# A graph-network kernel on one core: an order of work by tables, the low halves of a layer's rows on VectorE, and the sync queue in another order

## What is computed

```python
# layer 0: attention with 4 heads of 16, over the neighbours only
scores = einsum('bhnd,bhmd->bhnm', x @ Wself, x @ Wother)
masked = leaky_relu(a * scores, 0.2) / sqrt(16) + where(a == 0, -1e9, 0)
attn = softmax(masked, -1) * (a != 0)
x = layernorm(x + relu(attn @ (x @ Wv) + bias))
# layer 1: mean over the neighbours, adj with one more on the diagonal
x = layernorm(x + (adj + I) @ x / rowsum(adj + I))
# layer 2: adj @ (x @ W) + bias
x = layernorm(x + adj @ (x @ W2) + bias2)
# layer 3: 1 where adj @ x is over 0.5, else 0
t = adj @ x
x = layernorm(x + where(t > 0.5, 1, 0))
```

## Time and profile before

| | us |
|---|---|
| median of 3 runs | 1537.56 (1536.58 to 1537.99) |
| the profiled execution | 1541.21 |
| its span | 1539.1 |

### The profile page before, as it was taken

The page is one execution under the profiler, slowest core; times in us unless marked ns, Lnnn a source line. Parts: engine busy times, 40 slices in busy tenths (PEclk is TensorE's granted clock), DMA queues, the critical chain, the costliest instruction groups (busy, mean ns, idle before and its releaser), DMA issues.

```text
span 1539.1 us, 20977 instructions
## 1 busy us (share of the span) xinstructions
PE 1360.2 (88%) x7296; PEld 683.8 (44%) x7296; DVE 1240.7 (81%) x1490; ACT 1223.2 (79%) x1404; POOL 1053.1 (68%) x562
## 2 busy tenths in 40 slices
PE   4798898999999999999989989998999989799766
PEld 2443344454444444544444544444444444345323
DVE  2779889787979889788887879887788788987864
ACT  1699799887988889788888879888798888888631
POOL 3177768678677767777676786787677776876411
PEclk9999899999999999999999999999899999999977
DMA  6734444243333433343442443344334334101000
GB/s 94 117 34 75 47 87 52 58 39 60 77 44 69 48 67 73 48 58 34 98 51 58 40 62 75 44 74 45 67 55 67 53 37 82 41 15 28 14 11 11
DMA packets 140879, 84.95 MB, mean 55 GB/s; under 512 B 100372, under 2 KB 130522, under 8 KB 140762
## 3 DMA queue, kind: packets, MB, share of 16 engines
q1 hardware_dynamic: 125542, 64.67, 19.7%
q0 software_dynamic: 14160, 18.51, 15.4%
q10 hardware_dynamic: 1072, 0.43, 0.1%
HBM read 103.33 MB, written 21.38 MB: 81 GB/s over the span
## 4 chain that ended last, share of the span: by engine, by line
PE 50%; ACT 12%; issue 12%; DVE 12%; POOL 10%; DMA 2%; SPq 1%; ACTq 0%; POOLq 0%; DVEq 0%
PE M L604 10%; PE Z L570 9%; PE M L659 9%; PE Z L577 8%; POOL LS L503 7%; ACT LS L751 6%; PE Z L588 5%; ACT LS L759 4%; DVE LS L913 3%; PE Z L673 3%; DVE RP L899 3%; PE Z L613 3%; DMA adj_cast<-in_adj_dram 1%; PE Z L727 1%; DVE X L983 1%
## 5 line engine op out<-in xcount | busy, mean ns | idle before, releaser
L503 POOL TENSOR_TENSOR LS<-LS,MB 125x1000 f32<-125x1000 f32 x372 | 867.1, 2348 | 339.2 <-DVE LS L913 272.3
L751 ACT ACTIVATE LS<-Z 126x1000 f32<-126x1000 f32 x576 | 576.8, 1002 | 154.1 <-PE Z L577 153.1
L899 DVE TENSOR_TENSOR RP<-LS,RP 125x1000 f32<-125x1000 f32 x480 | 575.6, 1199 | 84.8 <-ACT LS L751 63.3
L759 ACT ACTIVATE LS<-LS 125x1000 f32<-125x1000 f32 x576 | 596.9, 1037 | 51.9 <-POOL LS L503 32.9
L570 PE MATMUL Z<-AT,BI 126*126 126x500 fp8e4 x1152 | 378.0, 411 | 79.1 <-ACT LS L751 52.5
L577 PE MATMUL Z<-FS,FO 128*125 128x500 f16 x1152 | 356.2, 391 | 0.0
L604 PE MATMUL M<-LS,V 126*18 126x500 f32 x2304 | 317.3, 624 | 5.9 <-ACT LS L759 5.8
L570 PEld LDWEIGHTS Z<-AT,BI 126*126 126x126 bf16 x1152 | 127.7, 142 | 389.9 <-ACT LS L751 187.1
L913 DVE TENSOR_TENSOR LS<-LS,MB 125x1000 f32<-125x1000 f32 x204 | 293.0, 1441 | 5.0
L577 PEld LDWEIGHTS Z<-FS,FO 128*125 128x125 f16 x1152 | 165.8, 144 | 97.4 <-issue 17.6
L659 PE MATMUL M<-AT,XP 125*128 125x500 fp8e4 x756 | 192.9, 377 | 0.0
(11 more groups left out here) (133 smaller groups left out, 811.2 us busy)
## 6 DMA issues: line engine op xcount, KB each, us to landing
MB<-row_maxima SPq DMA_DIRECT2D x48, 500.0 KB, 4.0
adj_cast<-in_adj_dram POOLq DMA_DIRECT2D x96, 183.1 KB, 4.5
FO<-PARTS SPq DMA_DIRECT2D x120, 46.9 KB, 2.2
FS<-PARTS SPq DMA_DIRECT2D x120, 46.9 KB, 2.1
XF<-in_x_dram SPq DMA_DIRECT2D x8, 336.0 KB
XA<-in_x_dram SPq DMA_DIRECT2D x8, 336.0 KB
out_dram<-X SPq DMA_DIRECT2D x7, 375.0 KB
AT<-adj_cast SPq DMA_TRANSPOSE x144, 2.8
```

Source lines behind the costliest of these rows:

```text
L503: nc.gpsimd.tensor_tensor(rows, rows, MB[:P, u % 2, :, :], ALU.subtract).then_inc(sub_pool, 1)
L751: nc.scalar.activation(LS[:PD, q % RL, :, :], banks("Z", q)[:PD], ACT.Prelu, alpha=SLOPE).then_inc(bent, 1)
L759: nc.scalar.activation(rows, rows, ACT.Exp, scale=0.25).then_inc(exps, 1)
L899: nc.vector.tensor_tensor(run, rows, run, ALU.max).then_inc(maxed, 1)
```

## The change

Each event of a graph gets its step from a table. Core of the diff (lines `...` left out):

```diff
-LAG = 18
-SUB_AT = LAG + 0
-EXP_AT = LAG + 2
-WEIGH_AT = LAG + 4
...
+POOL_AT, SUB_AT, EXP_AT, WEIGH_AT = 17, 18, 20, 22
+TURNED = (14, 14, 14, 14, 14, 14)
+MAXIMA = (14, 14, 14, 14, 14, 14)
+SPREAD = (17, 17, 17, 17, 17, 17)
+TAKE = (34, 34, 34, 34, 34, 34)
+SUMS = (35, 35, 34, 35, 35, 35)
+KEEP = (34, 35, 34, 35, 35, 35)
+MEANS = (25, 42, 60, 79)
+CENTRE = (26, 41, 62, 80)
+SQUARE = (27, 44, 63, 82)
...
+SCALE = (29, 46, 65, 83)
+HIGH = (30, 47, 66)
+LOW = (30, 47, 66)
+COLLECT = ((33, 34, 35, 36, 37, 38, 39, 40, 41),
...
+FEATURES = (15, 16, 18, 19, 20, 22, 26, 29, 31)
...
+LOADS = (53, 55, 57, 59, 58, 60, 61, 65, 29, 31, 30, 33)
+SLICES = ((7, 7, 7), (16, 17, 17), (49, 49, 49))
+ONES_AT = (10, 20, 51)
+HEADS_AT = ((7, 7), (10, 10), (39, 39), (41, 41))
+XF_AT, STORE_AT, XA_AT = 8, 11, 24
...
-TRANSPOSES = {3: 1, 15: 2, 47: 3}
-ONES_AFTER = 3
-FEATURES = {16: ("XT", 0), 17: ("FT", 0), 20: ("FE", 0), 21: ("XT", 1), 23: ("FT", 1), 25: ("FE", 1), 27: ("XT", 2), 28: ("FT", 2), 32: ("FE", 2)}
-MEANS = (25, 42, 61, 79)
-CENTRE, SQUARE, SUM, POWER, SCALE, HIGH, LOW, Y0, W0 = 1, 2, 2, 3, 4, 5, 5, 9, 12
...
-                if turned_at(q - 1) is not None:
-                    spread_maxima(turned_at(q - 1))
-                if slice_at(q):
-                    turn_slice(slice_at(q))
-                if slice_at(q - ONES_AFTER):
-                    add_ones(slice_at(q - ONES_AFTER))
...
+                u = turned_at(q, SPREAD, LAST_RT + 1)
+                if u is not None:
+                    spread_maxima(u)
+                for g, k in slice_at(q):
+                    turn_slice(g, k)
+                if ones_at(q) is not None:
+                    add_ones(ones_at(q))
+                for bb, h, side in parts_at(q):
+                    load_features(bb, h, side)
...
-            def low(b, l):
-                pool.wait_ge(xh_ready, 3 * b + l + 1)
-                nc.gpsimd.tensor_tensor(XP[:, :, F:2 * F], X[:, :, :], XP[:, :, 0:F], ALU.subtract).then_inc(xp_ready, 1)
...
+            def low_rows(b, l):
+                dve.wait_ge(xh_ready, 3 * b + l + 1)
+                nc.vector.tensor_tensor(XP[:, :, F:2 * F], X[:, :, :], XP[:, :, 0:F], ALU.subtract).then_inc(xp_ready, 1)
...
-                if q < QN and q % GROUP == 0:
-                    for n in range(GROUP):
-                        bend(q + n)
-                at = layer_at(q, HIGH)
-                if at and at[1] < 3:
-                    high(*at)
-                if unit_at(q, TAKE_AT) is not None:
-                    take(unit_at(q, TAKE_AT))
...
+                if layer_at(q, HIGH):
+                    high(*layer_at(q, HIGH))
+                if unit_at(q, TAKE) is not None:
+                    take(unit_at(q, TAKE))
+                if q < QN:
+                    bend(q)
```

More of the change, by code:

```diff
@@ L22 @@
 NF = len(TERMS)
-CUTS = 3
 KEEPS = 5
@@ L219, in adj_resnorm, with unit_at, turned_at @@
         block = ctx.enter_context(nc.Block())
-        def unit_at(q, at):
-            u, off = divmod(q - at, STEPS)
-            return u if off == 0 and 0 <= u < NU else None
-        def turned_at(q):
-            return NU - 1 if q == LAST_RT else unit_at(q, RT_AT) if q < LAST_RT else None
         def graph_at(q):
             return divmod(q, SPG)
+        def unit_at(q, steps):
+            for u in range(max(q // STEPS - 4, 0), min(q // STEPS + 1, NU)):
+                if STEPS * u + steps[u % UPG] == q:
+                    return u
+            return None
+        def turned_at(q, steps, last):
+            if q >= last:
+                return NU - 1 if q == last else None
+            u = unit_at(q, steps)
+            return u if u != NU - 1 else None
         def load_at(q):
@@ L244, in slice_at, with ones_at, parts_at, layer_at @@
             b, r = graph_at(q)
-            if r not in TRANSPOSES:
-                return None
-            g = NS * b + TRANSPOSES[r]
-            return g if g < NS * B else None
-        def layer_at(q, after):
-            for l, at in enumerate(MEANS):
-                b, off = divmod(q - at - after, SPG)
+            for s, steps in enumerate(SLICES):
+                for k, at in enumerate(steps):
+                    if at == r and NS * b + s + 1 < NS * B:
+                        yield NS * b + s + 1, k
+        def ones_at(q):
+            b, r = graph_at(q)
+            if r not in ONES_AT or NS * b + ONES_AT.index(r) + 1 >= NS * B:
+                return None
+            return NS * b + ONES_AT.index(r) + 1
+        def parts_at(q):
+            b, r = graph_at(q)
+            for n, steps in enumerate(HEADS_AT):
+                bb = b + (n >= 2)
+                for side in range(2):
+                    if steps[side] == r and bb < B:
+                        yield bb, (n + 2) % H, side
+        def layer_at(q, steps):
+            for l, at in enumerate(steps):
+                b, off = divmod(q - at, SPG)
                 if off == 0 and 1 <= b < B:
@@ L396, in _ @@
             sp.wait_ge(ones_in, 1)
-            turn_slice(0)
+            for k in range(CUT_Q):
+                turn_slice(0, k)
             add_ones(0)
```

202 lines of the change are left out of this document (101 added, 101 removed).

## The result

The changed kernel takes 1554.4 us (median of 4 runs, 1552.7 to 1556.1) against 1537.8 for the kernel before (4 runs, 1536.6 to 1542.9). The ratio is 1.0079, 95% interval 1.0048 to 1.0111: slower by 0.8%, where 1% faster was forecast. The time also lies 6 us above the upper end of the range. The profiled execution took 1556.13 us with a span of 1554.4, so it stands 15 above that of before, which is the size to explain, with the opposite sign to the sum of -15.

A forecast was written before the change was run, and what follows sets the result against it. No engine alone bounds the kernel: PE (88% busy) holds some units, a chain of other engines units 2 and 5. Terms 5 + 3 - 13 - 15 - 6 + 10 + 1 = -15 gave 1522.5 us (median), range 1503 to 1548.

The forecast's parts named there:

- What bounds the kernel: Over graph 4 PE idles at most 13.6 us; unit 3 is PE's, in units 2 and 5 PE waits for other engines.
- The rest: +1: keep, take and transposes in pieces: keep makes DVE's next maximum 1.2 us later, transposes nothing; +1 us (0 to +8).
- removes a wait for PE: ACT's take behind an exponential ends a wait for PE, at a place where PE is the bound; priced within +1 us.
- The high half: +10: ACT's high half ahead of a bend: longer waits for the scaling at layers 0 and 2; +10 us (0 to +20).
- layer 1 nothing: Within the high-half term, moving layer 1's high half ahead of the bend costs nothing.
- The low half: -15: Low half from POOL to DVE: ACT waits less for POOL's subtractions, 2.2 us a graph; -15 us (-19 to 0).
- Collecting earlier: -6: One step of four matmuls leaves each of units 3 and 0 for units 2 and 5; -6 us (-12 to 0).
- Centring: -13: Centring ahead of DVE's row maxima: ACT's 1.9 us wait at the square goes in 7 graphs; -13 us (-14 to -4).
- Next late is nothing: Once ACT's wait for the centring is gone, nothing else is late, as PE's feature matmul stood behind the same stall.
- The ones: +5 at the start, +3 in graph 1: Slice 1's ones issued behind feature loads and XF make PE wait: +5 us (+3 to +9), graph 1 +3 (0 to +4).
- DVE becomes the late one: Rival: DVE's low halves delay POOL, ACT's high half and bends; +32 us, 1554 at worst, 1545 at half; slower 0.26.
- its two signs: The rival holds if DVE's low half takes 2 us or more, or POOL's waits for DVE grow over 50 us.

The follow-up runs named there:

- e2: Changed kernel with ACT's copy of layer 1's third slice at step 58 instead of 59: 1534.1 us, 0.9973 of the kernel before.
- e7: Changed kernel with ones early, layer 1's last copy at 58 and its turn back at 60 instead of 59: 1524.4 us, 0.9895 of the kernel before.
- the base: The kernel before with only the low half of X moved from POOL to DVE; run twice, mean ratio taken as 0.9837 of the kernel before.
- e13: The base with layer 1's last turn back at 59, its copy's step, and unit 2's turned sums and keep at 58: 1530.0 us, 0.9934.
- e16: The base with ACT's take at a unit's step 34 ahead of the bend, not at 33 behind it: 1526.9 us, 0.9912.
- e17: The base with the features at the steps of the change, FT 2 at step 29: 1520.7 us, 0.9876.
- e14: The base with each layer's high half on ACT ahead of its step's bend: 1531.8 us, 0.9936.
- e6: Changed kernel with ones early and copy at 58, ACT's high half behind the bend again: 1541.0 us, 1.0010 of the kernel before.
- e5: Changed kernel with ones early and copy at 58, low half of X back on POOL: 1550.4 us, 1.0061 of the kernel before.
- e12: The kernel before with only the low half of X moved from POOL to DVE, first run: 1518.2 us, 0.9843.
- e18: The kernel before with only the low half of X on DVE, run again with more rounds: 1515.6 us, 0.9832.
- e11: e7's kernel with collecting, copying and layer 2's last turn back at the steps of before: 1534.1 us, 0.9934 of the kernel before.
- e9: e7's kernel with the centring behind the row maxima on DVE again, as before: 1528.4 us, 0.9912 of the kernel before.
- e19: The base with the centring ahead of the row maxima: 1515.9 us, 0.9842, beside 0.9832 for the base measured with it.
- e1: Changed kernel with the ones of slice 1 issued right behind its transposes again, ahead of feature loads and XF: 1548.1 us, 1.0057.

## Why the prediction was wrong, step by step

*What bounds the kernel: right, and incomplete.* PE is the bound of units 3 and 4, a chain of the other engines that of 2 and 5. But I took unit 4 for safe: a unit where "PE is the bound and nothing is won" is also a unit where every idle of PE is lost in full, and rows 2 left it out. The prediction read graph 4 and multiplied by seven; for graphs 0 and 1 it priced 8 us of its own, and 11 of the 15 us are lost there.

*The rest: +1, "nothing". This is the step that failed.* It held three edits by name and passed over a fourth. The fourth, the copy and the turn back of layer 1's last slice both at step 59, cost 25 us in the changed kernel (e2 16 for the copy, e7 9 for the turn back's place behind the turned sums) and 15 on the base (e13). It was to be read in the tables of the changed kernel, which the core of the diff leaves out: COPY has 59, BACK has 59, and in the other eight places a turn back stands one or two steps behind its copy. `take` ahead of the bend "removes a wait for PE"; it costs 11 us (e16). The features were not priced apart from FT 2, and cost up to 6 (e17). The transposes in pieces were not tested by themselves, nor was the order within a step on PE, where the turn back now stands ahead of the collecting.

*The high half: +10, right for the base, of the wrong sign for the changed kernel.* On the base it is +15 (e14), ACT's wait for the scaling goes from 9.2 to 19.7 us, and its places hold 10 of the 15; "layer 1 nothing" was wrong (0.4 a graph). In the changed kernel, for which the term was meant, undoing it costs 9 (e6): the wait falls as forecast, but the first collecting at 69 then waits for XP. Two edits that the sum priced apart depend on each other.

*The low half: -15, right.* 16 in e5, 24 to 26 alone on the kernel before (e12, e18), of which 17 are in the steps that the prediction named. Its duration was wrong: 2.23 us in the median where 0.95 to 1.1 was taken. The gain came all the same.

*Collecting earlier: -6, right as far as one difference of 6 us, good to 5, can tell* (e11).

*Centring: -13, wrong.* The 1.9 us were there and went (step 26 from 4.3 to 2.9), but the kernel gained 3 us in e9 and lost 1 in e19, neither told from nothing. "Next late is nothing" was the wrong sentence: in e9 DVE's scaling is late three steps on, by 1.0 us. On the base only 0.3 of the 1.4 are lost there; the rest went into steps 11, 23 and 71.

*The ones: +5 at the start, +3 in graph 1.* Both waits are in the trace. At the start PE waits until 67.06 instead of 55.30, 11.8 us, more than the upper end of 9, since the ones land 9.3 us behind their issue and not 3.4. The prediction had named this case beside its term: by the Trainium skill, "DMA: Bandwidth & Descriptors", Queues, rings and completion order, which has the descriptors of one issuing queue consumed in ring order on each DMA engine, the ones would land with XF. The 9.3 us agree with it; when XF itself landed, no row shows. In graph 1 PE waits 3.56 us, as worked out.

Yet putting the ones first again (e1) gave 3 us, not 15. In its trace step 12 of graph 0 begins at 58.2 instead of 69.0, but step 24 at 88.6 instead of 91.5: unit 1 gives 8 of the 11 us back. The windows of unit 1, the changed kernel first, then e1, show how:

```profile
69.02:91.50 22.48, 20.84 (x96) 11.80 (x94) 17.88 (x16) 18.03 (x23) 8.84 (x4) 0.96 0.22 47
```
```profile
58.20:88.60 30.40, 27.02 (x96) 15.00 (x94) 17.80 (x16) 18.31 (x22) 9.15 (x4) 0.71 0.52 96
```

The same 96 matmuls keep PE busy for 27.0 us at a mean granted clock of 0.71, and for 20.8 at 0.96. In the changed kernel the clock is at 0.50 from 53.6 to 70.7, mostly while PE stands idle, and at 1.00 from there on. In e1 PE starts early, waits 2.5 us for XF, and the clock is at 0.50 again from 65.6 to 79.2, in the midst of the work. So of the 8 us 6 are busy time at the lower clock and 2 are idle time: an earlier start was paid back in slower matmuls. The term had priced a wait, and not the clock behind it; why the clock falls again in e1 was not tested. Before, unit 1 takes 24.9 us (57.3 to 82.2).

*The rival "DVE becomes the late one" named 1554, and its two signs both came true*. Its own sum does not give that number: +32 on the median is 1570, and 1554 is what half of it gives. The signs: the low half takes 2.23 us, and POOL waits for DVE 312.5 us in graphs 1 to 7 instead of 254.8. Yet it is false: low halves on DVE are what the kernel gains by. Signs that a rival shares with a harmless outcome decide nothing; e5 and e12 do. That the measured time is the rival's number is luck.

*Added up.* From the base, 0.9837, to the changed kernel, 1.0079, are 37 us. The parts measured are 15 (copy and turn back), 15 (high half), 11 (`take`), 6 (features), 1 (centring), 3 (ones), -6 (collecting): 45. The other way, by the changed kernel itself, the ones, the copy and the turn back are 28 us (e7 is at 0.9895), which leaves 9 between e7 and the base; for these 9 the other parts, as measured mostly on the base, make 27. So the parts do not add: high half and collecting depend on each other, each part shifts where the clock is down, and each price is good to 5 to 7 us. What is shown is the sign and place of the copy and turn back in both kernels; how the rest divides is left open, and so are the loads of slice 2 at 58 to 65, and whether collecting early on the base would gain.

## What to carry to other kernels

When a table gives each event of a pipeline its step, check for every pair that hands data from one engine to another that the consumer's step is behind the producer's, above all where PE is the consumer and full; here one such pair cost 15 to 25 us, and nothing else in the change was found to cost more. Price moved events together where one waits for another, and ask of each removed wait where the same data is waited for next. Then try the one part with the clearest reason alone on the kernel before: here it was 1.6% faster, while the whole was 0.8% slower.
